# Attention of a fused two-layer kernel: the reciprocal of the softmax row sums moves from ScalarE (logarithm, exponential) to GpSimd (power of -1)

## The reference, cut to what matters

```python
attn = jnp.einsum('bqhd,bkhd->bhqk', q, k) * scale
attn = jnp.where(causal, attn, -jnp.inf)
attn = jax.nn.softmax(attn, axis=-1)
out = jnp.einsum('bhqk,bkhd->bqhd', attn, v).reshape(B, T, C)
```

## Time and profile before

| | us |
|---|---|
| median of 3 runs | 697.12 (695.51 to 697.45) |
| the profiled execution | 695.8 |
| its span in the trace | 694.0 |
| mean granted TensorE clock over the span | 0.941 of full speed |

### The profile page before, as it was taken

How to read it: one execution, slowest core, us unless ns; L and a number is a source line. 1 busy time by engine, 2 the same in 40 slices (tenths; PEclk the granted TensorE clock), 3 DMA queues, 4 the chain that set the end, 5 groups by cost and what they waited for, 6 DMA issues and landing times.

```text
span 694.0 us, 11004 instructions
## 1 busy us (share of the span) xinstructions
PE 617.2 (89%) x3252; PEld 436.7 (63%) x3252; DVE 549.1 (79%) x1350; ACT 491.1 (71%) x849; POOL 171.5 (25%) x143
## 2 busy tenths in 40 slices
PE   8788988998997899999999999782698599999996
PEld 4355555555544658888888887351385378888884
DVE  3657888888866758888888887756899589999997
ACT  5548999999743669999999998577544146666663
POOL 4222222222401405444555342310232000000000
PEclk9789999999997799999999999997698789999999
DMA  7000000000100030222102220000000212222201
GB/s 234 1 0 1 2 2 1 0 0 0 32 1 0 4 153 1 91 92 91 59 32 92 91 83 1 23 1 0 0 1 0 91 66 90 98 112 88 85 1 61
DMA packets 6797, 30.90 MB, mean 45 GB/s; under 512 B 906, under 2 KB 1043, under 8 KB 4435
## 3 DMA queue, kind: packets, MB, share of 16 engines
q1 hardware_dynamic: 6756, 30.42, 12.2%
HBM read 29.23 MB, written 1.19 MB: 44 GB/s over the span
## 4 chain that ended last, share of the span: by engine, by line
PE 71%; DVE 18%; ACT 5%; issue 3%; DMA 2%; SPq 0%; POOL 0%; DVEq 0%; ACTq 0%; POOLq 0%
PE PS L1102 16%; PE PS L1103 16%; PE PS L1104 16%; DVE STAT L779 5%; PE PS L1221 3%; PE PS L1183 3%; PE PS L1203 3%; PE PS L1217 2%; PE PS L1248 2%; PE PS L1182 2%; PE PS L1257 2%; PE PS L1128 2%; DVE HN L628 1%; DMA AR<-in_wmod 1%; DVE AR L1061 1%
## 5 line engine op out<-in xcount | busy, mean ns | idle before, releaser
L913 DVE TENSOR_TENSOR RA<-AR,RA 128x512 fp32r<-128x512 f32 x140 | 134.2, 982 | 29.2 <-ACT RA L499 28.4
L498 ACT ACTIVATE AR<-PS,BI 128x512 f32<-128x512 f32 x144 | 99.4, 690 | 26.2 <-PE PS L1104 16.6
L1102 PE MATMUL PS<-HH,WH 128*128 128x512 f32 x272 | 110.3, 406 | 7.8 <-DVE AR L1053 7.7
L1103 PE MATMUL PS<-HH,WL 128*128 128x512 f32 x272 | 108.6, 399 | 0.0
L1104 PE MATMUL PS<-HL,WH 128*128 128x512 f32 x272 | 108.4, 399 | 0.0
L499 ACT ACTIVATE RA<-PS,BI 128x512 fp32r<-128x512 f32 x144 | 98.4, 684 | 0.0
L779 DVE CUSTOM_DVE_ANT_0 STAT<-PS,MQ 128x128 f32<-128x128 f32 (+1 forms) x256 | 76.3, 354 | 20.7 <-PE PS L1204 20.3
L1102 PE MATMUL PS<-RA,WH 128*128 128x512 f32 x208 | 82.3, 396 | 2.5 <-DVE RA L1068 2.0
L1104 PE MATMUL PS<-RA,WH 128*128 128x512 f32 x208 | 81.5, 392 | 0.0
L1103 PE MATMUL PS<-RA,WL 128*128 128x512 f32 x208 | 81.4, 392 | 0.0
L303 POOL TENSOR_TENSOR AR<-AR 128x512 f32<-128x512 f32 x32 | 51.2, 1600 | 112.0 <-DVE AR L734 112.0
(11 more groups left out here) (185 smaller groups left out, 1183.4 us busy)
## 6 DMA issues: line engine op xcount, KB each, us to landing
AR<-comb SPq DMA_DIRECT2D x17, 1024.0 KB, 4.7
WS<-in_w SPq DMA_DIRECT2D x9, 512.0 KB, 5.4
WS<-in_w SPq DMA_DIRECT2D x8, 384.0 KB, 3.1
M<-in_mats SPq DMA_DIRECT2D x1, 1384.0 KB, 10.9
X<-in_xT SPq DMA_DIRECT2D x4, 256.0 KB, 4.4
out_xT<-X SPq DMA_DIRECT2D x4, 256.0 KB, 2.1
AR<-in_wmod SPq DMA_DIRECT2D x1, 768.0 KB, 8.1
KM<-in_kmats SPq DMA_DIRECT2D x1, 160.0 KB, 8.1
```

Source lines behind the costliest of these rows:

```text
L498: act.activation(G[:, c, :], PS[:, c, :], ACT.Gelu_apprx_tanh, bias=bias).then_inc(s["act"], 1)
L913: dve.tensor_tensor(out=GL[:, m0 % 2, c, :], in0=G[:, c, :], in1=f(GH[:, m0 % 2, c, :]), op=ALU.subtract).then_inc(s["lo"], 1)
L1102: pe.matmul(out, wh, xh, start=first, stop=False)
L1103: pe.matmul(out, wl, xh, start=False, stop=False)
```

## The change

The two activations per unit on ScalarE go, with the semaphore `ls_done` between them. GpSimd gets one `tensor_tensor` per unit with the operation `pow`: base `SU` (128 partitions by 256 elements, in place), exponent a constant column of -1 broadcast along the free axis. On GpSimd it stands ahead of the `join` of the same step; the last two stand behind the last join and ahead of `split_weights`. The constant costs one more `memset` of 128 by 1 at the start.

```diff
+            gp.memset(CON[:, 3:4], -1.0).then_inc(minus_done, 1)
...
             for n in range(3):
                 join(n)
+            def inverse_sum(n):
+
+                gp.wait_ge(su_done, n + 1)
+                gp.tensor_tensor(out=SU[:, n % 2, :], in0=SU[:, n % 2, :],
+                                 in1=CON[:, 3:4].to_broadcast([128, 256]), op=ALU.pow).then_inc(rsx_done, 1)
+
+            gp.wait_ge(minus_done, 1)
             for n in range(UNITS):
+                if n >= 2:
+                    inverse_sum(n - 2)
                 if n + 3 < UNITS:
                     join(n + 3)
+            inverse_sum(30)
+            inverse_sum(31)
             gp.wait_ge(moe[0]["w_in"], 16)
             split_weights(0, 0, 0, 1024)
...
-            def recip(n, n0):
-
-                act.wait_ge(su_done, n + 1)
-                act.activation(SU[:, n0 % 2, :], SU[:, n0 % 2, :], ACT.Ln).then_inc(ls_done, 1)
-                act.wait_ge(ls_done, n + 1)
-                act.activation(SU[:, n0 % 2, :], SU[:, n0 % 2, :], ACT.Exp, scale=-1.0).then_inc(rsx_done, 1)
-
             def step(n0, it=0):
...
                     evac_proj(n + 3, (n0 + 3) % 4)
-                if n0 >= 2:
-                    recip(n - 2, n0 - 2)
...
             evac_out(30, 30)
-            recip(30, 30)
             square(1, XC, 0)
             square(1, XC, 1)
             evac_out(31, 31)
-            recip(31, 31)
             inverse(1, 0)
```

More of the change, by code:

```diff
@@ L144, in build @@
         (proj_done, qk_evac, qx_ready, s_done, max_done, mp_ready, mt_done, qm_ready, st_done,
-         exp_done, pv_done, ot_done, su_done, ls_done, rsx_done, on_done, vx_ready, wo_done) = map(
+         exp_done, pv_done, ot_done, su_done, rsx_done, on_done, vx_ready, wo_done) = map(
             sem, ("proj_done", "qk_evac", "qx_ready", "s_done", "max_done", "mp_ready",
                   "mt_done", "qm_ready", "st_done", "exp_done", "pv_done", "ot_done", "su_done",
-                  "ls_done", "rsx_done", "on_done", "vx_ready", "wo_done"))
+                  "rsx_done", "on_done", "vx_ready", "wo_done"))
         l1_split = sem("l1_split")
@@ L152, in build @@
         bias_done = sem("bias_done")
+        minus_done = sem("minus_done")
         p1_psum, p1_done, a_done, sa_done, hsi_done, sqrt_done, s_ready, scan_done, hs2_mul, hs2_done = map(
```

## The result

The changed kernel takes 1918.41 us (median of 4 runs, 1917.66 to 1919.37) against 696.6 us before (with a fourth run beside the three of the table ahead): a ratio of 2.754, 95% interval 2.750 to 2.759. The forecast was 812 us with a range from 697 to 972. The direction was right; the size was out of all proportion.

What follows compares the result with a forecast made beforehand. TensorE and VectorE exchanging scores and maxima were taken to bound the kernel. Span 694.0 + 97.5 (steady part) + 18.6 (tail) = 810.1 us, with 1.8 around it 811.9; forecast 812 us, range 697 to 972.

Steps and rivals of the forecast that it cites:

- What bounds the kernel: Attention's steady part: TensorE and VectorE handing each other scores and maxima pace the 4.75 us round; ScalarE follows.
- Removal worth 0: Dropping Ln and Exp on ScalarE, 0.78 us per unit, gains 0 because the TensorE-VectorE round hides it.
- ScalarE paces the round: Rival: ScalarE's full queue sets the attention round, so removal saves up to 0.78 us a round; 678 us, chance 0.10.
- The price P = 6 us, at most 11: Time of one 128 by 256 power on GpSimd, estimated between 0.64 and 11 us from assumed elementary steps.
- very dear power: Rival: GpSimd's power takes over 11 us because its steps are not overlapped; over 970 us, chance 0.08.
- The page's 12 cycles per element for branching: Skill page's cost of data-dependent branching on GpSimd, giving 2.6 us per 256-column power; as a rival's price, 709 us.
- The stall by shared reading during a power: VectorE instructions reading only SBUF (lines 790, 792, 813) wait for the end of GpSimd's running instruction, powers included.
- P + 2.5: Forecast steady attention round in us: the power's time plus 2.5 for join, stalled VectorE lines, shuffle and hops.
- The rival without that stall: Rival: VectorE is not held during a power; round is power plus 1.4 us, 783 us total, inside the forecast's range.
- The form of the sum: Span before, plus 26 longer steady rounds, plus the tail; each microsecond of power beyond 6 costs 32 us.
- The threshold, 2.25 us: Power time on GpSimd above which the steady attention round grows beyond 4.75 us.
- The moved split, 2.2 us: First expert's weight split, now queued behind the last power, delays line 826 after the attention by 2.2 us.

## Why the prediction was wrong, step by step

- *What bounds the kernel:* right. TensorE and VectorE pace the round; with no inverse at all it is still 4.73 us.
- *Removal worth 0:* right, and the rival "ScalarE paces the round" is dead: the most there was to gain is about 3 us, and none of it in the rounds. That the term at the end was small and not zero (0.8 us seen there) changes nothing.
- *The price P = 6 us, at most 11:* **this is the step that failed.** It measured 41.13 us, 6.9 times as much. I bounded it from above by a count of 20 to 35 elementary steps at 0.31 us each, and that count stood in no row. What the runs put in its place is 0.159 us a column, as much as 41.13 / 0.31 = 133 of those passes: the count was short by a factor of four to seven. Nothing in the trace of before could have given it, and I should have carried "unbounded above" as a price instead of closing the range at 11. The rival "very dear power" had the right side and the right slope (32 us for each microsecond of P), with a chance of 0.08. Its reason, steps that are not overlapped, no run tests: what the power does inside its 0.159 us a column stays open. That the change came out slower, as I had said with 0.75, owes little to P = 6; any P over 2.5 us does that.
- *The page's 12 cycles per element for branching* (Trainium skill, GPSIMD Engine Reference, section 3.1) gave an estimate of 2.6 us. The measured 41.13 us is 16 times that, at the page's 1.2 GHz some 0.159 x 1200 = 190 cycles a column (an estimate). Whether branching has a part in it no run shows.
- *The stall by shared reading during a power:* wrong for the power, right for join and split. I generalised from additions, products and roundings to a power; that it reads little and computes for long would fit, but is not shown. My P + 2.5 came near partly because join, division and shuffle do stand in a row; the 0.3 us for lines 790 and 792 in it were not there. The rival without that stall had P + 1.4 for the round; it is P + 1.96, since it left out that the division waits for the join and the shuffle for the division. For 16 columns, where the join also meets line 792, it was P + 2.28. The Trainium skill (SBUF — State Buffer, section "SBUF: two separate sides") says that a GpSimd instruction that starts first gets the shared ports for the whole instruction; the 0.17 us of line 794 inside a power of 41.13 us differ, and the measurement decides.
- *The form of the sum:* right. With P = 41.13 in place of 6 it gives 810.1 + 32 x 35.13 = 1934 us of span against 1915.9; the 18 us between are mostly 27 rounds of 0.54 us less (14.6 us) and the 3.0 us behind line 828.
- *The threshold, 2.25 us:* near. At 1.64 us there is no loss; at 2.90 the round is 0.45 us longer, which puts the point at 4.73 - 2.28 = 2.45 us, by this working; no run has a P between the two.
- *The moved split, 2.2 us:* 2.0 in the traces with the multiplication, 1.9 in the changed kernel.
- *What I had not thought of:* TensorE's clock. Just past the threshold it costs more than the wait that brings it about (35 of the 53 us with 16 columns). In the changed kernel itself it hides behind the power, but for the 0.23 us that line 828 waits for the last output projection.

No version of these beats the kernel before by a sound margin: the ones that are ahead leave the inverse out.

## What to carry to other kernels

An engine's idle time is no room until the new operation's price is known on that engine: where the trace has no row for an operation, one instruction of it at the end of the same kernel gives the price per column, and a range without such a row has no upper end. Then ask what the removal can bring at most, by leaving the work out: here 3 us of 697 would have closed the case. When a kernel gets slower by more than the wait that was added, look at TensorE's granted clock before looking for a second wait, and try whether work that nobody reads brings the time back.

## What the runs showed of the hardware that I had not expected

- GpSimd's power takes 0.36 us + 0.159 us a column, within 6% whatever the values, the exponent's form or the number of partitions (64 columns: 10.51 us with 32, 10.55 with 128).
- It leaves VectorE's reads alone (0.17, 0.68 and 0.69 us beside it), while a GpSimd addition of 1.27 us turns 0.17 into 0.97 and 0.42 into 1.48 us.
- A GpSimd product of 256 columns by a broadcast column takes 0.62 us, about as much a column as its addition of two full operands (1.28 us for 512). One with two full operands, beside VectorE's work on SBUF, took 1.07 us, and the VectorE instructions there 1.11 and 1.22 instead of 0.69 and 0.68: the two engines stretched each other, in the one case that was measured.
- VectorE's reciprocal takes 1.75 us for 256 columns, where its product takes 0.42.
- With 16 columns of power TensorE went from full to half clock near 110 us, after rounds in which it was busy 85% of the time instead of 91%, and kept its clock when useless matmuls brought it back to 91%. Once at half it stayed there from 115 to 220 us, although it was busy for all of these 105 us. Four executions of that kernel had mean clocks from 0.833 to 0.880 (758.87 to 737.98 us), so how long it stood at half varied between them.
